# Softmax denominators issued pair by pair among the score matmuls of a causal attention layer

## The chip, the cores and the metric

The kernel runs on all 8 cores of one Trainium2 chip. Each core computes one element of a batch of 8, with the same program and no exchange between cores. The metric is device time in microseconds of the slowest core. Each core has a matrix engine (TensorE, PE in the profile; its weight loads are the rows PEld), a vector engine (DVE), a scalar engine (ACT), a general engine (POOL) and a queue engine for transfers (SP). Each engine takes its own instructions in program order, and they wait for each other through semaphores.

## The reference

Per batch element, x is 2048 tokens by 2048 features. The layer is, in short:

```
ln  = layernorm(x)
q,k,v = ln @ W_Q[h] + b, ln @ W_K[h] + b, ln @ W_V[h] + b      # 16 heads of 128
scores = q @ k.T / sqrt(128);  keys after the query are masked out
attn   = softmax(scores);      z = attn @ v
x  = x + layernorm(sum over heads of z @ W_O[h] + b_O)
bw = sign(weight) * mean(|weight|, per row)
x  = x + layernorm(layernorm(x) @ bw.T + bias)
```

The softmax divides exp(score) by the sum over all keys of a query. That sum, the denominator, is what the change is about.

## The kernel before, in words

The program has three stages. The first normalises and transposes x and makes q, k and v of head 0. The second runs through 16 heads. The third binarises the second weight and does the output projection and the feed-forward part. Only the second stage is touched.

A head is worked through in four blocks of 512 queries (`g` = 0 to 3, `GQ` = 512). Since keys after a query are masked, block g needs 4(g+1) chunks of 128 keys: 4, 8, 12 and 16 chunks, 40 in a head. For each chunk j there is:

- a **score** matmul (`emit_score`, L569), 128 keys by 512 queries. Chunks j = 0, 1 modulo 4 land in the two halves of the PSUM tensor psA, chunks 2, 3 modulo 4 in psB;
- an **exp** on ACT (`emit_exp`, L583), one for a pair of chunks, since it reads all of psA or all of psB (`estep` = 2). It writes the pair's slots of the SBUF buffer `ptil`. The score matmul that next writes the same half waits for it;
- for the last four chunks of a block, which are the diagonal ones (r = 0 to 3), a **mask** on POOL: a memset of the first r*128 columns (L606) and a multiplication of the next 128 by a triangle (L609);
- a **denominator** matmul (L619): a matrix of ones times the slot, accumulated over all chunks of the block in the second bank of psC. It waits for the chunk's exp, or for its mask where there is one.

After the last denominator matmul, ACT takes Ln (L624) and Exp (L628) to form the reciprocal, DVE multiplies each slot by it (L638), and PE multiplies the slots by v into psE (L656, the AV matmuls). In the fourth block 64 matmuls of the next head's q projection (L362) stand between the denominators and the AV matmuls, and hide the reciprocal.

The order of each engine's work is the order in which the Python code emits it; there is no scheduler. For PE it is, around a block: scores of the block's first four chunks, the AV matmuls of the block before, the rest of the scores, then all denominator matmuls of the block in one row. At the end of a head, q, k and v of the next come with 192 projection matmuls, with a short chain that forms the shift of the softmax (`emit_mh_mms`, `emit_mh_tail`, `emit_mb`) and 16 transposes of v.

Of the kernel before, what the change touches and what calls it, by code (L numbers as in the profile page):

```python
# [10 lines left out]
ALU = mybir.AluOpType  # L11
# [49 lines left out]
def build_program(SEQ, DM, H):  # L61
# [7 lines left out]
    TPG = min(4, NT)  # L69
    NG = NT // TPG  # L70
    GQ = TPG * 128
# [5 lines left out]
    p = Plan(nc)  # L77
# [26 lines left out]
    ptil = nc.alloc_sbuf_tensor("ptil", [128, max(NT * GQ, 4 * DM)], BF16)  # L104
    C2 = nc.alloc_sbuf_tensor("c2", [128, max(6 * DM, 4 * GQ + SEQ + 4 * DM)], BF16)
    eye_sb = nc.alloc_sbuf_tensor("eye_sb", [128, 128], BF16)
    tri_sb = nc.alloc_sbuf_tensor("tri_sb", [128, 128], BF16)
# [9 lines left out]
    onem_sb = nc.alloc_sbuf_tensor("onem_sb", [128, 128], BF16)  # L117
# [15 lines left out]
    pslot = [ptil[:, j * GQ:(j + 1) * GQ] for j in range(NT)]  # L133
# [18 lines left out]
    psC = nc.alloc_psum_tensor("psC", [128, 1024], F32)  # L152
# [21 lines left out]
    for dst, src in ((eye_sb, eye_h), (tri_sb, tri_h), (onec_sb, onec_h),  # L174
# [3 lines left out]
             inc="CONST", incn=16)  # L178
# [115 lines left out]
    sc_rinv_prev = 0  # L294
# [215 lines left out]
    def emit_mb(h):  # L510
        nonlocal pe_mb_prev, dv_mbias, dv_mbias_prev
        pe_mb = p.op("tensor", lambda e: e.matmul(
            psC[:, 0:1], oner_sb[:], nm_bf[:], start=True, stop=True),
            wait=[("DV", dv_nm_cur), ("DV", dv_qkv_evac_d[(h, 1)]),
                  ("SC", sc_rinv_prev)], inc="PE")
        pe_mb_prev = pe_mb
        dv_mbias = p.op("vector", lambda e: e.tensor_copy(
            mbias[:], psC[:, 0:1]), wait=[("PE", pe_mb)], inc="DV")
        dv_mbias_prev = dv_mbias

    for h in range(H):
# [10 lines left out]
        if h >= wo_start:  # L532
# [3 lines left out]
            for hh in range(hh0, min(hh0 + per, H)):  # L536
                p.op("gpsimd", lambda e, hh=hh: e.dma_start(
                    Bz[:, hh * DM:(hh + 1) * DM], wo_h.ap()[hh]),
                    inc="WO", incn=16)
# [8 lines left out]
        wait = [("DV", dv_qkv_all), ("DV", dv_mx_d[1])]  # L548
# [11 lines left out]
        estep = 2 if GQ == 512 else 1  # L560

        def emit_score(g, j, pe_sc):
            hb = j % 4
            wait = [("SC", psbuf_last_rd[hb])]
            if j == 0:
                wait += [("DV", dv_vch[h]), ("DV", dv_qkv_all)]
                if g == 0:
                    wait.append(("DV", dv_mx_d[1]))
            pe_sc[j] = p.op("tensor", lambda e, j=j, g=g, hb=hb: e.matmul(  # L569
                schalf[hb], kt_sb[:, j * 128:(j + 1) * 128],  # L570
                qt_sb[:, g * GQ:(g + 1) * GQ], start=True, stop=True),
                wait=wait, inc="PE")

        def emit_exp(g, j0, pe_sc, sc_exp):
            if estep == 2:
                buf = psA[:] if (j0 % 4 == 0) else psB[:]
                dst = ptil[:, j0 * GQ:(j0 + 2) * GQ]
            else:
                buf = schalf[j0 % 4]
                dst = pslot[j0]  # L580
            wait = [("PE", pe_sc[j0 + estep - 1]), ("DV", dv_mbias),
                    ("PE", max(ptil_slot_av[j0:j0 + estep]))]
            t_exp = p.op("scalar", lambda e, buf=buf, dst=dst: e.activation(  # L583
                dst, buf, AF.Exp, bias=mbias[:, 0:1], scale=C_ATTN),
                wait=wait, inc="SC")
            for jj in range(j0, j0 + estep):
                sc_exp[jj] = t_exp
                psbuf_last_rd[jj % 4] = t_exp

        pe_sc = {}  # L590
        sc_exp = {}
        mb_done = False
        for j in range(TPG):
            emit_score(0, j, pe_sc)
            if (j + 1) % estep == 0:
                if not mb_done:
                    emit_mb(h)
                    mb_done = True
                emit_exp(0, j + 1 - estep, pe_sc, sc_exp)
        for g in range(NG):  # L600
            chunks = (g + 1) * TPG
            gp_mask_j = {}
            for r in range(TPG):
                j = g * TPG + r
                if r > 0:
                    p.op("gpsimd", lambda e, j=j, r=r: e.memset(  # L606
                        ptil[:, j * GQ:j * GQ + r * 128], 0.0),
                        wait=[("SC", sc_exp[j])], inc="GP")
                gp_mask_j[j] = p.op("gpsimd", lambda e, j=j, r=r: e.tensor_tensor(  # L609
                    ptil[:, j * GQ + r * 128:j * GQ + (r + 1) * 128],  # L610
                    ptil[:, j * GQ + r * 128:j * GQ + (r + 1) * 128],
                    tri_sb[:], ALU.mult), wait=[("SC", sc_exp[j])], inc="GP")
            pe_den = 0
            for j in range(chunks):
                wait = [("SC", sc_exp[j])] if j < g * TPG else \
                    [("GP", gp_mask_j[j])]
                if j == 0:
                    wait.append(("SC", sc_rinv_prev))
                pe_den = p.op("tensor", lambda e, j=j, chunks=chunks: e.matmul(  # L619
                    psC[:, 512:512 + GQ], onem_sb[:], pslot[j],  # L620
                    start=(j == 0), stop=(j == chunks - 1)),
                    wait=wait, inc="PE" if j == chunks - 1 else None)
            p.drain("scalar")
            p.op("scalar", lambda e: e.activation(  # L624
                psC[:, 512:512 + GQ], psC[:, 512:512 + GQ], AF.Ln,
                bias=0.0, scale=1.0), wait=[("PE", pe_den)])
            p.drain("scalar")
            sc_rinv = p.op("scalar", lambda e, g=g: e.activation(  # L628
                rbc[g % 2], psC[:, 512:512 + GQ], AF.Exp, bias=0.0, scale=-1.0),
                wait=[("DV", rbc_war[g % 2])], inc="SC",  # L630
                lowp="softmax normalizer becomes a bf16 matmul operand")
            sc_rinv_prev = sc_rinv
            dv_norm = {}
            for j in range(chunks):
                wait = [("SC", sc_rinv)] if j == 0 else []
                if j == 0:
                    wait.append(("PE", pe_den))
                dv_norm[j] = p.op("vector", lambda e, j=j, g=g: e.tensor_tensor(  # L638
                    pslot[j], pslot[j], rbc[g % 2], ALU.mult),
                    wait=wait, inc="DV")  # L640
            rbc_war[g % 2] = dv_norm[chunks - 1]
            nchunks = (g + 2) * TPG
            if g + 1 < NG:
                pe_sc = {}
                for j in range(min(4, nchunks)):
                    emit_score(g + 1, j, pe_sc)
            elif h + 1 < H:
                emit_w_mms(h + 1, 0)
                emit_mh_sq(0, h + 1)
            pe_av = 0  # L650
            for j in range(chunks):
                wait = [("DV", dv_norm[j])]
                if j == 0:
                    wait += [("DV", dv_zevac.get(gidx - 1, 0)),
                             ("SC", max(sc_bw_evac_half))]
                pe_av = p.op("tensor", lambda e, j=j, chunks=chunks: e.matmul(  # L656
                    psE[:, 0:GQ], v_sb[:, j * 128:(j + 1) * 128], pslot[j],
                    start=(j == 0), stop=(j == chunks - 1)),
                    wait=wait, inc="PE")
                ptil_slot_av[j] = pe_av  # L660
            pe_av_all[h] = pe_av
            if g + 1 < NG:
                sc_exp = {}
                for j0 in range(0, min(4, nchunks), estep):
                    emit_exp(g + 1, j0, pe_sc, sc_exp)
                for j in range(min(4, nchunks), nchunks):
                    emit_score(g + 1, j, pe_sc)
                    if (j + 1) % estep == 0 and j + 1 > 4:
                        emit_exp(g + 1, j + 1 - estep, pe_sc, sc_exp)
            zpar = gidx % 2  # L670
            wait = [("PE", pe_av), (ZWs[zpar], zw_par_t[zpar])]
            dv_zevac[gidx] = p.op("vector", lambda e, zpar=zpar: e.tensor_copy(
                zstage[zpar], psE[:, 0:GQ]), wait=wait, inc="DV")
            zw_par_t[zpar] = p.op(
                "sync", lambda e, g=g, h=h, zpar=zpar: e.dma_start(
                    zs_h.ap()[g * TPG:(g + 1) * TPG, h].transpose([1, 0, 2]),
                    zstage[zpar].rearrange("p (t q) -> p t q", q=128)),
                wait=[("DV", dv_zevac[gidx])], inc=ZWs[zpar], incn=16)
            gidx += 1
            if g == NG - 1 and h + 1 < H:  # L680
                emit_mh_mms(0, h + 1)
# [243 lines left out]
    for i in range(NT):  # L925
# [6 lines left out]
        if i > 0:  # L932
# [5 lines left out]
         wait=[("OUT0", p.cnt("OUT0"))])  # L938
# [14 lines left out]
def _get_nc():  # L953
    key = (_SEQ, _DM, _H)
    if key not in _nc_cache:
        _nc_cache[key] = build_program(*key)
    return _nc_cache[key]
# [30 lines left out]
```

How the kernel before makes its waits and increments, by code:

```python
        def thunk(e, fn=fn, wait=wait, inc=inc, incn=incn, lowp=lowp):  # L43
            for (s, v) in wait:
                e.wait_ge(sems[s][0], v)
            if lowp is not None:
                with nc.allow_low_precision(reason=lowp):
                    ins = fn(e)
            else:
                ins = fn(e)
            if inc is not None:
                ins.then_inc(sems[inc][0], incn)
```

## Time and profile before

| | |
|---|---|
| median of 3 runs | 2399.13 us (2398.44 to 2399.26) |
| the profiled execution, its own time | 2399.46 us |
| its span, first to last instruction, slowest core | 2397.6 us |
| mean granted TensorE clock of that core | 0.906 |
| cores | 2387.9 to 2397.6 us |
| PE busy | 1860.8 us, 78% |
| DVE busy | 936.9 us, 39% |
| ACT busy | 614.4 us, 26% |
| POOL busy | 239.7 us, 10% |

In the span cut in 40 slices the heads fill slices 8 to 30 or so, with PE busy 70 to 80% there, ACT 10 to 40% and POOL at most 10%. PE busy is that of instructions which overlap in part: a 128x512 matmul is shown with 0.38 us at the full clock, yet the next one starts 0.22 us later. The granted clock has two levels in this trace, 1.00 (2.4 GHz) and 0.50 (1.2 GHz).

### The profile page before, as it was taken

The page shows a single profiled execution, that of the slowest core. Times are in us where ns is not written, and L with a number is a line of the kernel's source. Part 1 is how long each engine was busy: PE and PEld are TensorE (multiplying, and loading weights), DVE is VectorE, ACT ScalarE, POOL GpSimd, SP SyncE. Part 2 cuts the span into 40 slices and gives each one's busy share as a digit, 9 for nine tenths or more (in the row PEclk, how much of TensorE's full clock was granted, in tenths as well). Part 3 has the DMA queues.
Part 4 walks back from the last instruction along what each step waited for, and adds up shares of the span by engine and source line. Part 5 has one row for each costly group of instructions (what it writes and reads, how often), then busy time and mean ns, then how long its engine had stood idle before and what let it go on. Part 6 is the DMA issues. An engine that isn't in the chain of part 4 may idle for free.

```text
span 2397.6 us, 27121 instructions; the slowest of 8 cores (2387.9 to 2397.6 us)
## 1 busy us (share of the span) xinstructions
PE 1860.8 (78%) x8180; PEld 805.4 (34%) x8336; DVE 936.9 (39%) x1696; ACT 614.4 (26%) x785; POOL 239.7 (10%) x558
## 2 busy tenths in 40 slices
PE   1556877878778787787878879788744799999995
PEld 1232323323233232332323323233222344444442
DVE  3443333323233333333333333333243455555553
ACT  1134042240412304133141331403254311111111
POOL 1001010110111101111010111111110000000000
PEclk9778998989889898898988989889866899999997
DMA  6231211202122121221312234242054033333320
GB/s 153 89 84 18 29 23 16 29 12 29 16 22 25 16 30 16 23 25 14 31 16 22 25 49 47 35 55 45 5 180 149 18 88 88 88 88 88 88 76 39
DMA packets 178474, 119.33 MB, mean 50 GB/s; under 512 B 168100, under 2 KB 168100, under 8 KB 170148
## 3 DMA queue, kind: packets, MB, share of 16 engines
q0 software_dynamic: 107200, 75.51, 18.2%
q1 hardware_dynamic: 71140, 42.07, 7.0%
q8 instruction: 79, 1.29, 0.2%
q14 instruction: 55, 0.45, 0.1%
HBM read 125.97 MB, written 25.17 MB: 63 GB/s over the span
## 4 chain that ended last, share of the span: by engine, by line
PE 64%; ACT 11%; issue 9%; DVE 8%; POOL 4%; DMA 2%; DVEq 2%; ACTq 0%; POOLq 0%; another core or an unknown queue 0%; SPq 0%
PE psA L362 9%; PE psB L362 9%; PE psE L656 7%; ACT ptil L583 6%; PE psC L362 5%; PE psC L853 5%; PE psB L744 4%; PE psA L744 4%; PE psC L619 3%; POOL ptil L609 2%; PE psE L853 2%; PE psD L853 2%; PE psD L362 2%; PE psE L362 2%; DMA c<-x 2%
## 5 line engine op out<-in xcount | busy, mean ns | idle before, releaser
L638 DVE TENSOR_TENSOR ptil<-ptil,c 128x512 bf16<-128x512 bf16 x640 | 220.2, 417 | 479.6 <-ACT c L628 479.6
L362 PE MATMUL psA<-arena_a,wbuf 128*128 128x512 bf16 x1002 | 299.5, 384 | 6.8 <-ACT arena_a L276 3.8
L362 PE MATMUL psB<-arena_a,wbuf 128*128 128x512 bf16 x1002 | 298.6, 383 | 5.0 <-ACT arena_a L276 4.0
L656 PE MATMUL psE<-ptil,v 128*128 128x512 bf16 x625 | 185.1, 390 | 53.5 <-DVE ptil L638 53.3
L583 ACT ACTIVATE ptil<-psA,mbias 128x1024 bf16<-128x1024 f32 x160 | 178.3, 1114 | 182.9 <-PE psE L656 78.0
L619 PE MATMUL psC<-ptil,onem_sb 128*128 128x512 bf16 x624 | 179.7, 400 | 54.3 <-POOL ptil L606 25.2
L487 ACT ACTIVATE srow<-srow 1x1 f32<-1x1 f32 x32 | 6.5, 203 | 821.3 <-DVE srow L482 821.3
L609 POOL TENSOR_TENSOR ptil<-ptil,tri_sb 128x128 bf16<-128x128 bf16 x256 | 109.1, 426 | 890.0 <-ACT ptil L583 889.9
L583 ACT ACTIVATE ptil<-psB,mbias 128x1024 bf16<-128x1024 f32 x160 | 177.2, 1107 | 0.0
L569 PE MATMUL psA<-qt,kt 128*128 128x512 bf16 x314 | 107.3, 425 | 81.4 <-ACT ptil L583 50.9
L853 PE MATMUL psC<-arena_a,c 128*128 128x512 bf16 x496 | 149.9, 381 | 17.6 <-DVE c L837 9.2
L362 PE MATMUL psC<-arena_a,wbuf 128*128 128x512 bf16 x538 | 156.8, 381 | 4.9 <-DVE qt L376 4.5
L362 PEld LDWEIGHTS psA<-arena_a,wbuf 128*128 128x128 bf16 x1024 | 101.1, 99 | 131.2 <-issue 16.6
L362 PEld LDWEIGHTS psB<-arena_a,wbuf 128*128 128x128 bf16 x1024 | 100.9, 99 | 125.4 <-issue 8.6
L569 PE MATMUL psB<-qt,kt 128*128 128x512 bf16 x315 | 108.4, 428 | 26.2 <-ACT ptil L583 25.9
L656 PEld LDWEIGHTS psE<-ptil,v 128*128 128x128 bf16 x640 | 62.3, 97 | 187.9 <-issue 153.1
L619 PEld LDWEIGHTS psC<-ptil,onem_sb 128*128 128x128 bf16 x640 | 62.6, 98 | 174.3 <-issue 125.0
L853 PE MATMUL psE<-arena_a,c 128*128 128x512 bf16 x256 | 97.5, 381 | 0.1
L853 PE MATMUL psD<-arena_a,c 128*128 128x512 bf16 x255 | 97.1, 381 | 0.0
L362 PE MATMUL psD<-arena_a,wbuf 128*128 128x512 bf16 x235 | 89.5, 381 | 4.9 <-issue 3.2
L362 PE MATMUL psE<-arena_a,wbuf 128*128 128x512 bf16 x231 | 88.0, 381 | 0.3
L376 DVE TENSOR_SCALAR kt<-psD,bqkvT_sb 128x512 bf16<-128x512 f32 x15 | 11.3, 751 | 191.2 <-PE psC L362 191.2
(124 smaller groups left out, 2136.6 us busy)
## 6 DMA issues: line engine op xcount, KB each, us to landing
c<-fw POOLq DMA_DIRECT2D x16, 1024.0 KB, 5.1
ptil<-x SPq DMA_DIRECT2D x16, 1024.0 KB, 6.6
out<-wbuf POOLq DMA_DIRECT2D x16, 1024.0 KB, 9.2
wbuf<-wq POOLq DMA_DIRECT2D x16, 512.0 KB, 7.1
wbuf<-wk POOLq DMA_DIRECT2D x16, 512.0 KB, 7.1
c<-x SPq DMA_DIRECT2D x8, 1024.0 KB, 5.4
wbuf<-wv POOLq DMA_DIRECT2D x16, 512.0 KB, 7.1
zs<-c SPq DMA_DIRECT2D x64, 128.0 KB, 1.9
```

The lines of the kernel that those rows point to most:

```text
L362: e.matmul(banks[bidx], wslot[sl][:, c * 128:(c + 1) * 128], ln1t3[:, c, s * SLW:(s + 1) * SLW], start=(c == 0), stop=(c == NCH - 1)),
L376: e.tensor_scalar(d[:, s * SLW:(s + 1) * SLW], banks[bidx], bqkvT_sb[:, wi * H + h:wi * H + h + 1], None, ALU.add), wait=[("PE", pe_mm)],
L487: t_ln = p.op("scalar", lambda e, wh=which: e.activation(srow[0:1, 18 + wh:19 + wh], srow[0:1, 16 + wh:17 + wh], AF.Ln, bias=0.0, scale=1. ...
L569: pe_sc[j] = p.op("tensor", lambda e, j=j, g=g, hb=hb: e.matmul(schalf[hb], kt_sb[:, j * 128:(j + 1) * 128], qt_sb[:, g * GQ:(g + 1) * GQ] ...
L583: t_exp = p.op("scalar", lambda e, buf=buf, dst=dst: e.activation(dst, buf, AF.Exp, bias=mbias[:, 0:1], scale=C_ATTN), wait=wait, inc="SC")
L609: gp_mask_j[j] = p.op("gpsimd", lambda e, j=j, r=r: e.tensor_tensor(ptil[:, j * GQ + r * 128:j * GQ + (r + 1) * 128], ptil[:, j * GQ + r * ...
L619: pe_den = p.op("tensor", lambda e, j=j, chunks=chunks: e.matmul(psC[:, 512:512 + GQ], onem_sb[:], pslot[j], start=(j == 0), stop=(j == ch ...
L638: dv_norm[j] = p.op("vector", lambda e, j=j, g=g: e.tensor_tensor(pslot[j], pslot[j], rbc[g % 2], ALU.mult), wait=wait, inc="DV")
L656: pe_av = p.op("tensor", lambda e, j=j, chunks=chunks: e.matmul(psE[:, 0:GQ], v_sb[:, j * 128:(j + 1) * 128], pslot[j], start=(j == 0), st ...
L744: p.op("tensor", lambda e, hh=hh, s=s, d=zrd: e.matmul(projb[s], d[:, hh * 128:(hh + 1) * 128], Bz[:, hh * DM + s * 512:hh * DM + s * 512 ...
L853: p.op("tensor", lambda e, c=c, s=s: e.matmul(ffnb[s], ln3t[:, c * 128:(c + 1) * 128], bwt3[:, c, s * 512:s * 512 + PSW], start=(c == 0), ...
```

## The change

In both versions the exps, the masks, the reciprocal, the multiplications and the AV matmuls are the same instructions. The masks and the denominator matmuls are now emitted behind the exp of their own pair, by two new functions, `emit_mask` and `emit_den`, and `emit_emd`, which calls all three.

```diff
+        def emit_den(g, j, sc_exp, gp_mask_j):
+            chunks = (g + 1) * TPG
+            wait = [("SC", sc_exp[j])] if j < g * TPG else \
+                [("GP", gp_mask_j[j])]
+            if j == 0:
+                wait.append(("SC", sc_rinv_prev))
+            pe_den_d[g] = p.op("tensor", lambda e, j=j, chunks=chunks:
+                               e.matmul(psC[:, 512:512 + GQ], onem_sb[:],
+                                        pslot[j], start=(j == 0),
+                                        stop=(j == chunks - 1)),
+                               wait=wait,
+                               inc="PE" if j == chunks - 1 else None)
+
+        def emit_emd(g, j0, pe_sc, sc_exp, gp_mask_j):
+            emit_exp(g, j0, pe_sc, sc_exp)
+            for jj in range(j0, j0 + estep):
+                if jj >= g * TPG:
+                    emit_mask(g, jj, sc_exp, gp_mask_j)
+                emit_den(g, jj, sc_exp, gp_mask_j)
...
-                emit_exp(0, j + 1 - estep, pe_sc, sc_exp)
+                emit_emd(0, j + 1 - estep, pe_sc, sc_exp, gp_mask_j)
         for g in range(NG):
             chunks = (g + 1) * TPG
-            gp_mask_j = {}
-            for r in range(TPG):
...
-            pe_den = 0
-            for j in range(chunks):
...
+            pe_den = pe_den_d[g]
...
                 for j0 in range(0, min(4, nchunks), estep):
-                    emit_exp(g + 1, j0, pe_sc, sc_exp)
+                    emit_emd(g + 1, j0, pe_sc, sc_exp, gp_mask_j)
                 for j in range(min(4, nchunks), nchunks):
                     emit_score(g + 1, j, pe_sc)
                     if (j + 1) % estep == 0 and j + 1 > 4:
-                        emit_exp(g + 1, j + 1 - estep, pe_sc, sc_exp)
+                        emit_emd(g + 1, j + 1 - estep, pe_sc, sc_exp,
+                                 gp_mask_j)
```

The waits of each instruction are as before. On ACT, DVE, POOL and SP the order of the instructions is as before too; only PE's order differs. On PE, first in the first two blocks of head 0 before (L551 the transposes of v, L569 scores, L512 the shift, L619 denominators, L656 AV matmuls):

```order
L551 MATMUL psA<-eye_sb,ptil 128x128 x16
L569 MATMUL psA<-qt,kt 128x512 x2
L512 MATMUL psC<-nm_bf,oner_sb 128x1
L569 MATMUL psB<-qt,kt 128x512 x2
L619 MATMUL psC<-ptil,onem_sb 128x512 x4
L569 MATMUL psA<-qt,kt 128x512 x2
L569 MATMUL psB<-qt,kt 128x512 x2
L656 MATMUL psE<-ptil,v 128x512 x4
L569 MATMUL psA<-qt,kt 128x512 x2
L569 MATMUL psB<-qt,kt 128x512 x2
L619 MATMUL psC<-ptil,onem_sb 128x512 x8
```

The same place on PE now (L608 is the denominator matmul, L669 the AV matmul):

```order
L569 MATMUL psA<-qt,kt 128x512 x2
L512 MATMUL psC<-nm_bf,oner_sb 128x1
L608 MATMUL psC<-ptil,onem_sb 128x512 x2
L569 MATMUL psB<-qt,kt 128x512 x2
L608 MATMUL psC<-ptil,onem_sb 128x512 x2
L569 MATMUL psA<-qt,kt 128x512 x2
L569 MATMUL psB<-qt,kt 128x512 x2
L669 MATMUL psE<-ptil,v 128x512 x4
L608 MATMUL psC<-ptil,onem_sb 128x512 x4
L569 MATMUL psA<-qt,kt 128x512 x2
L608 MATMUL psC<-ptil,onem_sb 128x512 x2
L569 MATMUL psB<-qt,kt 128x512 x2
```

Each pair of denominator matmuls stands directly behind the scores that feed its exp, and ahead of the next pair of scores. The four denominators of a block's first four chunks, whose scores are issued ahead of the AV matmuls, come together behind those.

On PE at the end of the fourth block, before, where the last scores, the row of denominators and the first projection matmuls (L362) of the next head stand:

```order
L569 MATMUL psA<-qt,kt 128x512 x2
L569 MATMUL psB<-qt,kt 128x512 x2
L619 MATMUL psC<-ptil,onem_sb 128x512 x16
L362 MATMUL psA<-arena_a,wbuf 128x512 x2
L362 MATMUL psB<-arena_a,wbuf 128x512 x2
```

The same place on PE now:

```order
L608 MATMUL psC<-ptil,onem_sb 128x512 x2
L569 MATMUL psA<-qt,kt 128x512 x2
L608 MATMUL psC<-ptil,onem_sb 128x512 x2
L569 MATMUL psB<-qt,kt 128x512 x2
L608 MATMUL psC<-ptil,onem_sb 128x512 x2
L362 MATMUL psA<-arena_a,wbuf 128x512 x2
```

The row of 16 is gone: two denominators stand at its place, and the others alternate with pairs of scores through the block.

## Rows read from the trace of the kernel before

**Rows 1.** The page: chain that ended last by engine; denominator matmuls.
```profile
PE 64%; ACT 11%; issue 9%; DVE 8%; POOL 4%; DMA 2%; DVEq 2%; ACTq 0%; POOLq 0%; another core or an unknown queue 0%; SPq 0%
...
L619 PE MATMUL psC<-ptil,onem_sb 128*128 128x512 bf16 x624 | 179.7, 400 | 54.3 <-POOL ptil L606 25.2
```

**Rows 2.** Timeline, fourth block: start, duration (us), engine, line, operation, [idle before <-releaser].
```profile
527.63 3.62 PE L656 MATMUL psE<-ptil,v 128*128 128x512 bf16 x11 [1.26 <-DVE ptil L638]
...
531.42 0.59 PE L569 MATMUL psA<-qt,kt 128*128 128x512 bf16 x2 [0.17 <-issue]
...
532.22 1.11 ACT L583 ACTIVATE ptil<-psA,mbias 128x1024 bf16<-128x1024 f32 x1 [1.77 <-PE psA L569]
...
533.48 0.59 PE L569 MATMUL psA<-qt,kt 128*128 128x512 bf16 x2 [1.03 <-ACT ptil L583]
...
536.98 3.61 PE L619 MATMUL psC<-ptil,onem_sb 128*128 128x512 bf16 x16
537.35 1.11 ACT L583 ACTIVATE ptil<-psB,mbias 128x1024 bf16<-128x1024 f32 x1
...
539.59 0.43 POOL L609 TENSOR_TENSOR ptil<-ptil,tri_sb 128x128 bf16<-128x128 bf16 x1
...
540.69 0.58 ACT L624 ACTIVATE psC<-psC 128x512 f32<-128x512 f32 x1 [2.23 <-PE psC L619]
540.71 0.59 PE L362 MATMUL psA<-arena_a,wbuf 128*128 128x512 bf16 x2
```

**Rows 3.** Timeline, first block of the same head.
```profile
500.01 1.12 ACT L583 ACTIVATE ptil<-psA,mbias 128x1024 bf16<-128x1024 f32 x1 [4.30 <-DVE mbias L517]
...
501.82 0.41 POOL L609 TENSOR_TENSOR ptil<-ptil,tri_sb 128x128 bf16<-128x128 bf16 x1
...
503.84 0.58 PE L619 MATMUL psC<-ptil,onem_sb 128*128 128x512 bf16 x1 [0.16 <-POOL ptil L609]
...
504.22 1.06 PE L569 MATMUL psA<-qt,kt 128*128 128x512 bf16 x2
...
505.07 1.06 PE L569 MATMUL psB<-qt,kt 128*128 128x512 bf16 x2
```

**Rows 4.** Timeline, second block, and the ends of the third.
```profile
508.38 1.11 ACT L583 ACTIVATE ptil<-psB,mbias 128x1024 bf16<-128x1024 f32 x1
...
508.63 0.59 PE L569 MATMUL psA<-qt,kt 128*128 128x512 bf16 x2 [0.69 <-ACT ptil L583]
...
510.44 1.11 ACT L583 ACTIVATE ptil<-psB,mbias 128x1024 bf16<-128x1024 f32 x1
...
512.68 0.42 POOL L609 TENSOR_TENSOR ptil<-ptil,tri_sb 128x128 bf16<-128x128 bf16 x1
...
513.25 0.38 PE L619 MATMUL psC<-ptil,onem_sb 128*128 128x512 bf16 x1 [0.36 <-POOL ptil L609]
...
515.87 2.61 PE L656 MATMUL psE<-ptil,v 128*128 128x512 bf16 x8 [1.26 <-DVE ptil L638]
...
525.00 0.38 PE L619 MATMUL psC<-ptil,onem_sb 128*128 128x512 bf16 x1 [0.37 <-POOL ptil L609]
```

**Rows 5.** Stretches: busy us of each engine (instructions), granted clock, DMA share, GB/s.
```profile
core 2: us, PE busy (x) PEld busy (x) DVE busy (x) ACT busy (x) POOL busy (x), PEclk, DMA share, GB/s
502.00:506.50 4.50, 3.84 (x8) 0.85 (x8) 0.51 (x2) 1.31 (x3) 1.67 (x5) 0.50 0.00 0
506.60:508.00 1.40, 1.27 (x4) 0.38 (x4) 0.82 (x3) 0.63 (x1) 0.00 (x0) 1.00 0.00 0
532.00:534.00 2.00, 0.97 (x5) 0.19 (x2) 0.45 (x1) 1.78 (x2) 0.00 (x0) 1.00 0.27 61
558.00:561.00 3.00, 1.53 (x5) 0.38 (x4) 2.76 (x4) 0.00 (x0) 0.00 (x0) 1.00 1.56 152
561.20:564.50 3.30, 3.30 (x9) 1.26 (x9) 1.25 (x3) 0.20 (x1) 0.00 (x0) 0.50 0.23 34
564.60:566.00 1.40, 1.40 (x8) 0.62 (x7) 0.00 (x0) 0.00 (x0) 0.00 (x0) 1.00 0.00 0
```

More of the change, by code:

```diff
@@ L588, in emit_exp, with emit_mask @@
                 psbuf_last_rd[jj % 4] = t_exp
+        def emit_mask(g, j, sc_exp, gp_mask_j):
+            r = j - g * TPG
+            if r > 0:
+                p.op("gpsimd", lambda e, j=j, r=r: e.memset(
+                    ptil[:, j * GQ:j * GQ + r * 128], 0.0),
+                    wait=[("SC", sc_exp[j])], inc="GP")
+            gp_mask_j[j] = p.op("gpsimd", lambda e, j=j, r=r: e.tensor_tensor(
+                ptil[:, j * GQ + r * 128:j * GQ + (r + 1) * 128],
+                ptil[:, j * GQ + r * 128:j * GQ + (r + 1) * 128],
+                tri_sb[:], ALU.mult), wait=[("SC", sc_exp[j])], inc="GP")
+        def emit_den(g, j, sc_exp, gp_mask_j):
[16 more added lines that the diff above has]
+                emit_den(g, jj, sc_exp, gp_mask_j)
         pe_sc = {}
         sc_exp = {}
+        gp_mask_j = {}
+        pe_den_d = {}
         mb_done = False
@@ L598, in build_program @@
                     mb_done = True
-                emit_exp(0, j + 1 - estep, pe_sc, sc_exp)
+                emit_emd(0, j + 1 - estep, pe_sc, sc_exp, gp_mask_j)
         for g in range(NG):
             chunks = (g + 1) * TPG
-            gp_mask_j = {}
-            for r in range(TPG):
[L604 to L612, printed above, removed]
-            pe_den = 0
-            for j in range(chunks):
[L615 to L622, printed above, removed]
+            pe_den = pe_den_d[g]
             p.drain("scalar")
@@ L663, in build_program @@
                 sc_exp = {}
+                gp_mask_j = {}
                 for j0 in range(0, min(4, nchunks), estep):
-                    emit_exp(g + 1, j0, pe_sc, sc_exp)
+                    emit_emd(g + 1, j0, pe_sc, sc_exp, gp_mask_j)
                 for j in range(min(4, nchunks), nchunks):
```

## The prediction

> **What bounds the kernel now.** I read the chain of waits first. Two thirds of it are PE, 11% ACT and 4% POOL, and DMA is 2% [rows 1]: the kernel is bound by PE's queue and by the places where that queue stands waiting, not by transfers. Then I read the timeline of one head, which the 16 heads repeat, at the places where PE waits within the attention blocks.
>
> In the fourth block [rows 2] the reader is to see two engines that overlap. ACT starts its exps 1.03 us apart ((537.35 - 532.22)/5). PE needs 0.59 us for the pair of scores that feeds one, and then idles: 1.03 us ahead of the pair at 533.48, which waits for the exp that frees psA. Two score buffers are enough to keep ACT fed, since the next scores are made in one while ACT reads the other. Behind the last scores the 16 denominator matmuls run without a gap, in 3.61 us, or 0.216 us each. They end at 540.59, and PE goes on with the next head at 540.71. So PE's queue alone sets the pace from here. The last mask ended at 540.02, so that not even a PE with nothing else to do could have ended the denominators much before 540.5.
>
> In the first two blocks the last denominator waits for POOL's last mask: it starts at 503.84 and 513.25, each time behind a mask, as the third block's at 525.00 does [rows 3, 4]. The row of denominators costs hardly anything on the path there.
>
> **The change part by part.** PE takes its matmuls in the order written. The work on every engine is the same as before: 640 denominator matmuls and 640 scores. What is added is a wait in a bad place: a denominator pair waits for the exp (or the mask) of the scores directly ahead of it, and the next scores are queued behind it, though their buffer is free. ACT waits for those scores. The overlap of scores with exps is gone for every pair but the first two of a block.
>
> The step that takes its place, at the full clock, from [rows 2]: two scores until the end of the second, 0.59; to ACT's start 0.21 (532.22 - 532.01); exp 1.11; back to PE 0.15 (533.48 - 533.33); two denominators issued, 0.43. That is 2.49 us a pair, against the 1.03 us of ACT's pace and the pair's 0.43 us in the row of denominators behind.
>
> A diagonal pair waits for its mask. For r = 0, 1 the second mask ends 1.10 us behind the exp (501.82 + 0.41 against 500.01 + 1.12) [rows 3]; for r = 2, 3 it is 1.55 us (512.68 + 0.42 against 510.44 + 1.11) [rows 4]. PE starts some 0.12 us after a mask. The first diagonal pair takes 0.59 + 0.21 + 1.11 + 1.10 + 0.12 + 0.22 = 3.35 us, the last, to the end of its last matmul, 0.59 + 0.21 + 1.11 + 1.55 + 0.15 + 0.38 = 3.99 us.
>
> From the end of the AV matmuls of the block before to the end of the last denominator:
>
> - Fourth block: four denominators 0.86, four plain steps 9.96, the diagonal ones 3.35 and 3.99: 18.2 us. Before: 531.25 to 540.59 = 9.3. Added: 8.8.
> - Third block: 0.86 + 4.98 + 3.35 + 3.99 = 13.2 us. Before: 518.48 to 525.38 = 6.9. Added: 6.3.
> - Second block: the denominators of chunks 2 and 3 wait for the exp that ends at 509.49, so scores that ran at 508.63 start at 509.64 + 0.43 = 510.07; the two diagonal pairs lead to 517.4. Before: 513.63. Added: 3.8 [rows 4].
> - First block, at the low clock (issue 0.43 a matmul, a pair of scores 1.06, from [rows 3]): the second denominator starts behind the mask at about 502.35; scores 502.8 to 503.8, exp 504.0 to 505.1, mask until 506.7, last denominator until 507.3. Before: 504.42. Added: 2.9.
>
> That is 21.8 us a head, with nothing beside it: in the first three blocks reciprocal, DVE and AV matmuls hang on the last denominator, and in the fourth the 64 projection matmuls are queued behind it on PE. The later start of an AV row hides nothing. Sixteen heads: 349 us. POOL's weight loads are queued behind the masks of the head before and so come later with everything else; transfers have no part in the chain worth a price here.
>
> **The clock.** TensorE's granted clock is at 0.50 through 502 to 506.5 although PE is busy 3.84 of 4.50 us, and rises only then; it is 1.00 from 558 to 561, with PE busy 1.53 of 3.00 us (some five matmuls), and is at 0.50 right behind [rows 5]. At 532 to 534 PE was busy 0.97 of 2.00 us and kept the full clock. A step of the new order has four matmuls, some 1.2 of 2.49 us, 48% in this measure, just where rows of both kinds stand; the diagonal steps have about 35%. So I expect falls within the blocks. At the low clock a step is 1.06 + 0.21 + 1.11 + 0.15 + 0.86 = 3.39 us, 0.90 more, with PE busy about 60% of it, less than the 85% that went ahead of the rise. Once fallen, the clock then stays low until the AV row or the projections. There are 12 steps in the last three blocks. I take four of them at the low clock: 3.6 us. The projections behind the fourth block mostly start at the low clock and need what those behind 561.2 needed, about 3.3 us at half pace, which loses 1.7 us. Together 5.3, and so 27.1 us a head, 434 us in all.
>
> The page "TensorE: Matmul & The Clock Gate" of the Trainium skill (Part 1, and "HAM oscillation") has a rule that speaks for less: it ties the fall to a stretch in which the engine is idle throughout. No part of the new blocks is such a stretch, since each step has four matmuls, so by that rule the clock stays up. The fall behind 561 is against it, since PE had five matmuls in the 3 us before. By that rule alone the time would be that of the second case below.
>
> The sum is made against the profiled execution, 2399.5 us (span 2397.6), which is 0.3 us above the median of the runs. 2399.5 + 434 = 2833 us.
>
> The bounds: all 12 steps at the full clock and the projections too, 349 us, 2748 us. All 12 at the low clock: 10.8 + 1.7 for the projections, and 2.6 us for the three rows of four denominators, 36.9 us a head, 590 us, 2990 us. I stay near the middle of the lower half, since each AV row is dense and gives the full clock back to the steps behind it.
>
> **The rivals.**
>
> 1. The serial order as above, the clock falls for part of the steps: 2833 us, 2770 to 2900. For it: the order of PE, and the rows of the clock.
> 2. The same, but the clock stays at its upper level: 2748 us (2735 to 2770). For it: 532 to 534. Against it: the fall behind 561 and the sparse diagonal steps.
> 3. The same, but the low clock nearly throughout, which also slows the AV rows: 2900 to 2990 us. Against it: at 506.6 the clock is up just as an AV row begins, and it would be so again.
> 4. The other side: the denominators fill the gaps in which PE waits for ACT. That needs PE to go on with the next scores while a denominator waits, from the moment at which scores can be started ahead of a waiting matmul. Each gap has 1.03 us of idle time and a pair needs 0.43. But the price is small even then: masks end at 540.02, the denominator behind them at 540.02 + 0.12 + 0.38 = 540.52 instead of 540.59, and the other blocks wait for masks already, so 0.07 us a head, 1 us. Only an earlier rise of the clock in the first block could add to that, by 1.7 us a head, which is 27 us: 2371 to 2399 us. Against it: in all rows a waiting matmul holds those behind it, as the scores at 533.48 hold the row of denominators, whose first twelve inputs were ready long before. The same page (Part 2, on loading the stationary operand) says that only weight loads are pulled ahead and matmuls stay in program order, with which these rows agree.
> 5. The order doesn't change what it says: PE's order shows that it does, so this has no chance of its own.
>
> **How the numbers follow.** Case 1 has 0.80, case 2 has 0.10, case 3 has 0.07, case 4 has 0.03. The time is that of case 1, 2833 us. A range of 2745 to 2900 holds cases 1 and 2 nearly whole. All cases but the fourth are far slower than before; about 0.2% (5 us) is what a measurement can tell from no change. Slower: 0.97. Within 0.2%: 0.01. Faster: 0.02.
>
> **What would show it.** In the changed kernel's fourth block ACT's exps should start some 2.5 us apart at the full clock and 3.4 at the low one, not 1.03, each releasing a denominator matmul (L608) that is followed by two scores (L569) without a wait. The wait of ACT for PE's scores should rise to hundreds of microseconds. POOL's diagonal masks should release denominators with scores behind them. The mean granted clock should fall from 0.906 to about 0.83. A head should take some 27 us longer, with the growth largest in its fourth block. If exps stay 1.03 us apart, the first term is wrong; if the steps are 2.5 us but the granted clock stays near 0.9, case 2 holds.

## The result and the profile after

The changed kernel is slower. Its median is 2859.8 us over 10 runs, that of the kernel before 2399.2 us over 10 runs beside it; the ratio is 1.192, with a 95% interval of 1.190 to 1.193. The forecast was 2833 us, in a range of 2745 to 2900. (In some executions the cores of one or both dies show a lower granted clock than the others and take longer; the ratios, and the medians given below, leave these out.)

| | before | after |
|---|---|---|
| span of the profiled execution, us | 2397.6 | 2856.8 |
| PE busy, us | 1860.8 (78%) | 2028.6 (71%) |
| mean granted clock, slowest core | 0.906 | 0.806 |
| ACT's share of the chain that ended last | 11% | 14% |

The page of the changed kernel shows the chain by engine, and then the groups for denominators, exps and scores (count, then busy us, mean ns of one, then idle us ahead of them and what ended most of it):

```profile
PE 63%; ACT 14%; issue 8%; DVE 7%; POOL 4%; DMA 2%; DVEq 1%; ACTq 1%; POOLq 0%; SPq 0%
...
L608 PE MATMUL psC<-ptil,onem_sb 128*128 128x512 bf16 x640 | 273.8, 491 | 459.7 <-ACT ptil L583 164.9
...
L583 ACT ACTIVATE ptil<-psA,mbias 128x1024 bf16<-128x1024 f32 x160 | 178.3, 1114 | 341.9 <-PE psA L569 180.0
L583 ACT ACTIVATE ptil<-psB,mbias 128x1024 bf16<-128x1024 f32 x160 | 177.9, 1112 | 255.4 <-PE psB L569 255.4
...
L569 PE MATMUL psA<-qt,kt 128*128 128x512 bf16 x320 | 142.5, 540 | 27.0 <-DVE v L557 27.0
...
L569 PE MATMUL psB<-qt,kt 128*128 128x512 bf16 x320 | 147.5, 557 | 0.0
```

The same groups for exps and scores before:

```profile
L583 ACT ACTIVATE ptil<-psA,mbias 128x1024 bf16<-128x1024 f32 x160 | 178.3, 1114 | 182.9 <-PE psE L656 78.0
...
L583 ACT ACTIVATE ptil<-psB,mbias 128x1024 bf16<-128x1024 f32 x160 | 177.2, 1107 | 0.0
L569 PE MATMUL psA<-qt,kt 128*128 128x512 bf16 x314 | 107.3, 425 | 81.4 <-ACT ptil L583 50.9
...
L569 PE MATMUL psB<-qt,kt 128*128 128x512 bf16 x315 | 108.4, 428 | 26.2 <-ACT ptil L583 25.9
```

PE's idle time ahead of denominators was 54.3 us [rows 1] and is 459.7 us, 405 us more. Part of that replaces waits that stood ahead of scores, 108 us before and 27 now. All in all PE is not busy for 828 us of the span instead of 537, which is 291 us of the loss; the other 168 us are its busy time, which grew though the work is the same. ACT's exps are as fast as before (1.11 us), but they wait 435 us for scores; the exps from psB had no wait at all before. A denominator matmul's mean went from 400 to 491 ns, which is the clock: one alone is shown with 0.38 us at the full clock and with 0.58 or 0.59 at the low one.

The timeline of a fourth block shows the cycle (start, duration, engine, operation, idle time before and what ended it; weight loads and transfers are left out). It answers to [rows 2].

```profile
634.62 0.59 PE L569 MATMUL psA<-qt,kt 128*128 128x512 bf16 x2
635.43 1.11 ACT L583 ACTIVATE ptil<-psA,mbias 128x1024 bf16<-128x1024 f32 x1 [2.27 <-PE psA L569]
636.68 0.59 PE L608 MATMUL psC<-ptil,onem_sb 128*128 128x512 bf16 x2 [1.47 <-ACT ptil L583]
637.12 0.59 PE L569 MATMUL psB<-qt,kt 128*128 128x512 bf16 x2
637.92 1.11 ACT L583 ACTIVATE ptil<-psB,mbias 128x1024 bf16<-128x1024 f32 x1 [1.38 <-PE psB L569]
639.17 1.01 PE L608 MATMUL psC<-ptil,onem_sb 128*128 128x512 bf16 x2 [1.47 <-ACT ptil L583]
...
641.25 1.11 ACT L583 ACTIVATE ptil<-psA,mbias 128x1024 bf16<-128x1024 f32 x1 [2.22 <-PE psA L569]
...
644.58 1.11 ACT L583 ACTIVATE ptil<-psB,mbias 128x1024 bf16<-128x1024 f32 x1 [2.22 <-PE psB L569]
...
654.73 0.58 PE L608 MATMUL psC<-ptil,onem_sb 128*128 128x512 bf16 x1 [0.16 <-POOL ptil L596]
655.27 1.01 PE L362 MATMUL psA<-arena_a,wbuf 128*128 128x512 bf16 x2
```

The reader is to see a loop of two engines, each of which now waits for the other: PE 1.47 us for the exp, ACT 1.38 us for the scores. From 635.43 to 637.92 is 2.49 us, the step of the prediction. From 641.25 to 644.58 it is 3.33 us. The clock has fallen by then: the pair at 639.17 takes 1.01 us instead of 0.59. The projections at 655.27 still run at the low clock.

The stretches of the same head, from the second block on, cut where the granted clock changes (busy us of PE, its weight loads, DVE, ACT and POOL with the number of instructions, then the clock, the share of the DMA engines and GB/s):

```profile
597.40:604.10 6.70, 3.17 (x12) 0.96 (x10) 0.69 (x1) 3.17 (x3) 0.95 (x3) 1.00 0.10 22
604.20:610.90 6.70, 3.93 (x9) 1.13 (x10) 1.73 (x6) 2.29 (x3) 1.44 (x4) 0.50 0.01 1
611.00:617.70 6.70, 3.96 (x16) 1.34 (x14) 1.64 (x4) 3.95 (x4) 0.00 (x0) 1.00 0.08 20
617.90:631.40 13.50, 8.19 (x18) 2.24 (x19) 2.15 (x7) 3.93 (x6) 2.39 (x7) 0.50 0.00 0
631.50:638.20 6.70, 4.74 (x19) 1.63 (x17) 2.55 (x7) 3.05 (x4) 0.00 (x0) 1.00 0.08 20
638.30:658.70 20.40, 12.12 (x27) 3.52 (x28) 1.82 (x6) 6.37 (x7) 3.54 (x8) 0.50 0.14 14
658.80:661.00 2.20, 2.20 (x12) 0.98 (x10) 2.20 (x8) 0.00 (x0) 0.00 (x0) 1.00 1.06 104
```

In each of these three blocks the clock came up while the AV matmuls of the block before ran (from 609.85 and 629.92, and those of the first block) and fell a few steps later. In the steps at the low clock PE is busy about 60% of the time and the clock stayed low; it rose again where matmuls followed each other closely.

Where the time went, by the starts of ACT's first exp and its four Ln's in each head, mean of the first 15 heads over the 8 cores:

| us a head | before | after | growth |
|---|---|---|---|
| first exp to Ln of block 1 | 4.5 | 7.5 | 3.0 |
| to Ln of block 2 | 9.4 | 13.6 | 4.2 |
| to Ln of block 3 | 11.8 | 20.0 | 8.2 |
| to Ln of block 4 | 15.2 | 27.1 | 11.9 |
| to the first exp of the next head | 59.8 | 61.3 | 1.5 |

The sum of the growths is 28.8 us, and 16 heads make 461 us.

### The profile page after: what moved, and what is told of

Same layout as the page of the kernel before. It is cut to its first block, busy times and chain, and to the rows that moved or that the text cites. A ratio compares the mean times of both kernels' runs of the same rounds, so it can differ in the third digit from the quotient of the medians.

```text
span 2856.8 us, 27277 instructions; the slowest of 8 cores (2847.5 to 2856.8 us)
## 1 busy us (share of the span) xinstructions
PE 2028.6 (71%) x8336; PEld 827.9 (29%) x8336; DVE 936.9 (33%) x1696; ACT 630.2 (22%) x785; POOL 239.4 (8%) x558
## 4 chain that ended last, share of the span: by engine, by line
PE 63%; ACT 14%; issue 8%; DVE 7%; POOL 4%; DMA 2%; DVEq 1%; ACTq 1%; POOLq 0%; SPq 0%
ACT ptil L583 10%; PE psA L362 8%; PE psB L362 8%; PE psC L608 7%; PE psE L669 5%; PE psC L362 4%; PE psA L759 4%; PE psC L868 4%; PE psB L759 4%; PE psB L569 3%; PE psA L569 3%; POOL ptil L596 2%; PE psE L868 2%; PE psD L868 2%; PE psD L362 2%
## 5 line engine op out<-in xcount | busy, mean ns | idle before, releaser
L608 PE MATMUL psC<-ptil,onem_sb 128*128 128x512 bf16 x640 | 273.8, 491 | 459.7 <-ACT ptil L583 164.9
L362 PE MATMUL psA<-arena_a,wbuf 128*128 128x512 bf16 x1024 | 320.1, 401 | 3.1 <-ACT arena_a L276 3.1
L362 PE MATMUL psB<-arena_a,wbuf 128*128 128x512 bf16 x1024 | 317.4, 398 | 3.2 <-ACT arena_a L276 3.2
L608 PEld LDWEIGHTS psC<-ptil,onem_sb 128*128 128x128 bf16 x640 | 64.3, 100 | 686.8 <-issue 675.5
L669 PE MATMUL psE<-ptil,v 128*128 128x512 bf16 x640 | 189.2, 429 | 28.6 <-DVE ptil L651 28.6
L569 PE MATMUL psA<-qt,kt 128*128 128x512 bf16 x320 | 142.5, 540 | 27.0 <-DVE v L557 27.0
L362 PE MATMUL psC<-arena_a,wbuf 128*128 128x512 bf16 x544 | 157.2, 379 | 4.5 <-DVE qt L376 4.5
L569 PE MATMUL psB<-qt,kt 128*128 128x512 bf16 x320 | 147.5, 557 | 0.0
L362 PEld LDWEIGHTS psA<-arena_a,wbuf 128*128 128x128 bf16 x1024 | 104.2, 102 | 140.4 <-issue 32.7
L362 PEld LDWEIGHTS psB<-arena_a,wbuf 128*128 128x128 bf16 x1024 | 104.4, 102 | 136.4 <-issue 26.6
L669 PEld LDWEIGHTS psE<-ptil,v 128*128 128x128 bf16 x640 | 64.5, 101 | 175.9 <-issue 140.6
L362 PE MATMUL psD<-arena_a,wbuf 128*128 128x512 bf16 x240 | 90.9, 379 | 4.5 <-issue 3.6
L362 PE MATMUL psE<-arena_a,wbuf 128*128 128x512 bf16 x240 | 90.9, 379 | 0.0
L759 PE MATMUL psA<-arena_b,kt 128*128 128x512 bf16 x256 | 77.9, 386 | 3.4 <-ACT c L782 3.4
```

Of the source, the lines that this page charges most:

```text
L362: e.matmul(banks[bidx], wslot[sl][:, c * 128:(c + 1) * 128], ln1t3[:, c, s * SLW:(s + 1) * SLW], start=(c == 0), stop=(c == NCH - 1)),
L608: e.matmul(psC[:, 512:512 + GQ], onem_sb[:], pslot[j], start=(j == 0), stop=(j == chunks - 1)),
L759: p.op("tensor", lambda e, hh=hh, s=s, d=zrd: e.matmul(projb[s], d[:, hh * 128:(hh + 1) * 128], Bz[:, hh * DM + s * 512:hh * DM + s * 512 ...
```

## The experiments

In all of them `emit_emd` of the changed kernel is edited. In all but one, a list `pend` holds the denominators that are not yet issued, and `flush_den(keep)` issues all but the last `keep` pairs; it is called with 0 at a block's end. The one without it adds matmuls instead.

```diff
-                emit_den(g, jj, sc_exp, gp_mask_j)
+                pend.append((g, jj, sc_exp, gp_mask_j))
+            flush_den(KEEP)
+        def flush_den(keep):
+            while len(pend) > keep * estep:
+                emit_den(*pend.pop(0))
```

**Denominators two pairs late** (`KEEP` = 2).

> Each denominator pair is issued two pairs later than in the changed kernel: behind the scores of the pair after next's exp buffer, so that its exp is done when PE comes to it; the last two pairs stand at the block's end. As many denominators are interleaved as two fewer pairs a block allow. Theory (the wait ahead of the next scores is the cause, not the interleaving): exps are 1.03 us apart again, the last denominator ends 0.5 us behind the last mask as before; 2395 to 2405 us. Rival (interleaving itself costs, by switching PE between two kinds of matmuls and two PSUM banks): each of 12 pairs a head between scores keeps a cost of at least 0.2 us, 192 pairs, so over 2435 us.

Measured: ratio to before 1.0067 (1.0050 to 1.0084), median 2413.9 against 2397.7 us. The wait is gone and with it 96% of the loss. The rival's cost of 0.2 us a pair is not there: in the trace one, three and five pairs of denominators stand between scores in blocks 2, 3 and 4, 144 in all (the expectation's 192 count those behind a block's last scores too), and they would have cost 29 us. But 16 us are left, and 2414 lies above the theory's 2405. The cores of this run tell where they come from (span, mean granted clock):

```profile
core 0: 2410.7 us, clock 0.892
...
core 4: 2403.2 us, clock 0.897
core 5: 2395.6 us, clock 0.906
core 6: 2391.6 us, clock 0.906
...
```

Time follows the clock: the two cores at 0.906, the value of before, have spans of 2391.6 and 2395.6 us, like those of before (2387.9 to 2397.6). The same stretch of one head on core 0, and below it on core 6:

```profile
707.40:714.10 6.70, 4.33 (x17) 1.44 (x16) 0.69 (x1) 4.37 (x5) 2.40 (x7) 1.00 0.09 20
714.30:720.90 6.60, 5.79 (x15) 1.79 (x14) 3.46 (x9) 3.12 (x5) 0.00 (x0) 0.50 0.01 2
```

```profile
708.20:714.90 6.70, 4.49 (x17) 1.53 (x16) 0.69 (x1) 4.53 (x5) 2.39 (x7) 1.00 0.09 20
715.10:721.70 6.60, 5.17 (x20) 1.92 (x20) 3.46 (x9) 4.60 (x5) 0.00 (x0) 1.00 0.10 22
```

Almost the same work goes ahead in both; on core 0 the clock falls as the second block's reciprocal is made, and the next stretch does 15 matmuls instead of 20. So on core 6 the interleaving costs nothing that can be told from noise: a head takes 100.8 us there and 100.7 before. A likely reason for the fall on core 0, not tested by itself, is that the interleaving takes matmuls out of the row that had stood ahead of that gap.

**Denominators one pair late** (`KEEP` = 1).

> Each denominator pair is issued one pair later than in the changed kernel, behind the next pair of scores. Theory: the chain from one exp to the one that uses the same buffer becomes 1.11 + 0.15 + 0.43 (denominators) + 0.59 + 0.21 = 2.49 us for two pairs, 1.25 us a pair where ACT alone needs 1.03; 0.22 us for some 10 to 12 pairs a head and 16 heads: 35 to 42 us, 2430 to 2450 us. No diagonal wait is ahead of scores, and the clock stays up as before. Rival (interleaving itself costs): as for the version with two pairs, the same in both.

Measured: 2464.1 us, a single execution and so without an interval, with cores from 2450.7 to 2462.5 us. That is 14 us over the expected 2450. A stretch of the fourth block on core 0 has the period of the theory:

```profile
650.89 1.11 ACT L583 ACTIVATE ptil<-psA,mbias 128x1024 bf16<-128x1024 f32 x1 [2.36 <-PE psA L569]
...
652.15 0.59 PE L608 MATMUL psC<-ptil,onem_sb 128*128 128x512 bf16 x2 [0.60 <-ACT ptil L583]
652.58 0.59 PE L569 MATMUL psA<-qt,kt 128*128 128x512 bf16 x2
...
653.38 1.11 ACT L583 ACTIVATE ptil<-psA,mbias 128x1024 bf16<-128x1024 f32 x1 [0.37 <-PE psA L569]
...
655.87 1.11 ACT L583 ACTIVATE ptil<-psA,mbias 128x1024 bf16<-128x1024 f32 x1 [0.37 <-PE psA L569]
```

The exps into the same buffer are 2.49 us apart (650.89, 653.38, 655.87), two pairs as expected, and the scores between them do not wait for a mask. A head takes 105.0 us on this core against 100.7 before, so 4.3 us where 2.6 was expected. The clock, assumed to stay up, did not: the trace's clock record has 2.3, 1.8 and 2.7 us a head more of blocks 2 to 4 at the low level than before on the same core. At half pace these 6.8 us can hold at most 3.4 us of lost work; how much of them is on the path was not measured. Of the 4.3 us, 0.7 lie behind the fourth Ln, where the theory had none, and stay unexplained.

**Extra matmuls in the gaps of the changed kernel**, to keep PE active.

```diff
+            if g > 0 and j0 >= 4:      # psD <- qt,kt, 128x512, results unread
+                emit_fill(3 if j0 < g * TPG else (4 if j0 == g * TPG else 5))
+            for jj in range(j0, j0 + estep):
                 emit_den(g, jj, sc_exp, gp_mask_j)
```

> The changed kernel with extra matmuls, whose results nobody reads, into the unused PSUM tensor psD while PE would wait for an exp or a mask: 3 ahead of a plain denominator pair, 4 and 5 ahead of the diagonal ones, in blocks 2 to 4 only, 48 a head. Theory (7 us a head of the loss is the low clock that the sparse steps bring): steps stay 2.49 us, the clock stays at its upper level through the blocks, the projections behind the fourth block start fast; 2735 to 2765 us, some 110 us faster than the changed kernel although PE has 768 matmuls more. Rival (the steps are longer for another reason, or the clock falls all the same): no faster than 2860 us, and up to 40 us slower.

Measured: ratio 1.1514 (1.1474 to 1.1554), which is 2761 us; the fastest run is 2752.6 us. The edit adds 9, 15 and 21 matmuls in blocks 2, 3 and 4, so 45 a head and 720 in all, not the 48 and 768 of the expectation (the trace shows 718). In the profiled execution six of the eight cores have 2744.3 to 2752.5 us. The other two, cores 6 and 7, have 2773 us, by three heads with 65 to 68 us from the fourth Ln to the next exp instead of 59.8. Their granted clock shows why. For 251 us in all, 135 of them in these three stretches, it stood at a third value, 0.81, which no other core of this run had. The stretch from 1370 to 1424 us on core 6 and, below it, on core 5:

```profile
1370.00:1424.00 54.00, 50.10 (x186) 20.37 (x188) 15.80 (x26) 0.20 (x1) 2.29 (x2) 0.81 0.24 24
```

```profile
1370.00:1424.00 54.00, 45.43 (x209) 20.25 (x207) 18.92 (x32) 1.09 (x4) 2.29 (x2) 0.93 0.21 22
```

Core 6 does 186 matmuls where core 5 does 209. What brought that value is not known. Adding work made the kernel some 98 us faster by the ratio, and 107 us by the fastest run. The third block on core 0, where every step has the full clock:

```profile
589.77 1.11 ACT L583 ACTIVATE ptil<-psA,mbias 128x1024 bf16<-128x1024 f32 x1 [1.38 <-PE psA L569]
591.03 0.59 PE L614 MATMUL psC<-ptil,onem_sb 128*128 128x512 bf16 x2 [0.82 <-ACT ptil L583]
591.46 0.59 PE L569 MATMUL psB<-qt,kt 128*128 128x512 bf16 x2
591.89 0.81 PE L592 MATMUL psD<-qt,kt 128*128 128x512 bf16 x3
592.26 1.11 ACT L583 ACTIVATE ptil<-psB,mbias 128x1024 bf16<-128x1024 f32 x1 [1.38 <-PE psB L569]
...
594.75 1.11 ACT L583 ACTIVATE ptil<-psA,mbias 128x1024 bf16<-128x1024 f32 x1 [1.38 <-PE psA L569]
```

The exps stay 2.49 us apart (589.77, 592.26, 594.75), and PE's wait is 0.82 us instead of 1.47 because three unread matmuls (L592) fill the rest. The four blocks of a head (the first four lines of the table above) now grow, against before on the same core, by 3.0, 4.0, 6.2 and 9.1 us, and the fifth line by nothing. With the clock up through blocks 3 and 4 that measures the serial part nearly alone: 22.3 us a head, where the prediction had 21.8.

**Only the fourth block interleaved** (`KEEP` = 0 in block 4, 99 elsewhere).

> Only the fourth block of each head interleaved as in the changed kernel; the first three with the row of denominators as before. Theory (each block pays its own price): the fourth block's 12.0 us and 1.5 us of slow projections a head, 16 heads, 216 us: 2600 to 2630 us. Rival (the blocks act on each other, the clock of one falling into the next, so that one alone costs much less than its share): under 2590 us.

Measured: ratio 1.0886 (1.0870 to 1.0902), 2609.5 us. The fourth block takes 26.7 us from Ln to Ln and the way to the next exp 61.4, about as in the changed kernel, with 27.1 and 61.3; the first three are those of before within 0.3 us. The blocks pay separately.

**Plain denominators at once, diagonal ones at the block's end** (`KEEP` = 0 for pairs without a mask, 99 for those with one).

> Plain denominators (no mask) issued at once as in the changed kernel, the four diagonal ones of a block in a row at its end, where their masks hold no scores. Theory, by the terms of the prediction: the first block is as before; second block +1.4 us; third 0.86 + 2 x 2.49 + 0.80 + 1.11 + 1.03 + 2.08 = 10.9 us against 6.9, +4.0; fourth 15.8 against 9.3, +6.5; 11.9 us a head, and 2 to 5 us for the low clock: 2399 + 16 x 13.9 to 16.9 = 2620 to 2670 us. So the mask waits would be worth some 190 to 240 us of the 460. Rival (the mask waits count little, since masks are waited for at a block's end in any order): over 2750 us.

Measured: ratio 1.1015 (1.0978 to 1.1052), which is 2643 us. So 217 us of the 460 come from diagonal denominators that stood ahead of scores, and the loss of the first block is all of that kind. The expectation calls this the worth of the mask waits, which is too much. The edit takes away the wait for the diagonal pair's exp too, and the low clock of a core goes from 1082 to 1106 us down to 727 to 751. What the mask adds to a step can be read in the changed kernel, at the first diagonal pair of the head above:

```profile
600.03 0.59 PE L569 MATMUL psA<-qt,kt 128*128 128x512 bf16 x2
...
603.40 0.59 PE L569 MATMUL psB<-qt,kt 128*128 128x512 bf16 x2
```

The step is 3.37 us instead of 2.49, so 0.88 us more, four times a head. By my estimate from these two numbers the masks alone are some 56 us of the 217. ACT's exps in a fourth block of this run:

```profile
704.39 1.11 ACT L583 ACTIVATE ptil<-psA,mbias 128x1024 bf16<-128x1024 f32 x1 [2.79 <-PE psA L569]
706.88 1.11 ACT L583 ACTIVATE ptil<-psB,mbias 128x1024 bf16<-128x1024 f32 x1 [1.38 <-PE psB L569]
709.37 1.11 ACT L583 ACTIVATE ptil<-psA,mbias 128x1024 bf16<-128x1024 f32 x1 [1.38 <-PE psA L569]
711.86 1.11 ACT L583 ACTIVATE ptil<-psB,mbias 128x1024 bf16<-128x1024 f32 x1 [1.38 <-PE psB L569]
715.19 1.11 ACT L583 ACTIVATE ptil<-psA,mbias 128x1024 bf16<-128x1024 f32 x1 [2.21 <-PE psA L569]
716.21 1.11 ACT L583 ACTIVATE ptil<-psB,mbias 128x1024 bf16<-128x1024 f32 x1
```

Three plain steps are 2.49 us long, the one to 715.19 is 3.33 (low clock), and the last exp follows after 1.02 us, since nothing waits between the diagonal pairs.

**The rows of before, with extra matmuls where PE waits.** These are put ahead of a head's scores too, into psD, from operands that don't change in this stage (`onem_sb` and `arena_a`). `emit_warm(n)` emits n of them: 10 behind the projection matmuls of v, 3 ahead of the transposes of v, 6 behind these, 4 ahead of block 1's denominators, and 2, 4 and 4 behind the first scores of blocks 2, 3 and 4.

```diff
             emit_w_mms(h, 2)
+            emit_warm(10, [("DV", dv_qkv_evac_d[(h, 1)])])
...
+            emit_warm(3)
...
+        emit_warm(6, [("SC", sc_evacA[NT - 1])])
...
+            if g == 0:
+                emit_warm(4)
...
+                emit_warm(2 if g == 0 else 4)
```

> The kernel before (rows of denominators at a block's end) with extra matmuls, whose results nobody reads, into the unused psD while PE waits: 10 and 3 around the norm matmuls of k, 6 ahead of a head's scores, 4 ahead of the first block's denominators, 2, 4 and 4 while the reciprocal is made. Theory (the low clock at a head's start costs PE time on the path: 16 transposes at 0.12 us and the scores and denominators of block 1 at half pace): the clock stays up through a head's start, 15 to 25 us less than before: 2375 to 2390 us. Rival (the extra matmuls delay what follows them, or the clock falls there all the same): 2399 us or more.

Measured: ratio 0.9933 (0.9911 to 0.9956), median 2383.6 us. Faster than before by 0.7%, 16 us by the ratio, as expected. The low clock adds up to 201 to 263 us a core instead of 434 to 451. Where the time came from is not what the theory said. From a fourth Ln to the next first exp a head has 58.8 us where before has 59.8, and that is the whole gain. The first block, now nearly always at the full clock, goes from 4.50 to 4.33 us, the second from 9.43 to 9.33, and the fourth grows by 0.3. The end of a first block on core 7, all of it at the full clock, shows why so little:

```profile
494.82 0.42 POOL L606 TENSOR_TENSOR ptil<-ptil,tri_sb 128x128 bf16<-128x128 bf16 x1
...
495.39 0.38 PE L618 MATMUL psC<-ptil,onem_sb 128*128 128x512 bf16 x1 [0.36 <-POOL ptil L606]
...
495.86 0.58 ACT L656 ACTIVATE psC<-psC 128x512 f32<-128x512 f32 x1 [2.17 <-PE psC L618]
```

The last denominator still waits for the last mask, as in [rows 3]; only its own 0.58 us became 0.38.

**Two pairs late, with the same extra matmuls.**

> The version with denominators two pairs late and the same extra matmuls. Theory (what that version lost, 15 us, was only the clock's fall in the third block of some cores; its wait costs nothing): as the rows with the same extra matmuls within 5 us, 2372 to 2392 us, on all cores alike. Rival (the interleaving costs by itself): 12 us or more above them.

Measured: ratio 0.9918 (0.9897 to 0.9939), median 2380.3 us, the fastest version here. The 16 us that this order lost without them are gone. The expectation wanted all cores alike, and they are not: their spans go from 2361.3 to 2376.5 us, with clocks from 0.958 to 0.943. The interval overlaps that of the one above, so which of the two orders is better is open; against before both are faster, by under 1%.

## Why the prediction was right, point by point

**What bounds the kernel, and the serial step.** Right. The step is 2.49 us at the full clock, and each of PE and ACT waits for the other in it. The prediction's 2.9, 3.8, 6.3 and 8.8 us for the four blocks are 3.0, 4.0, 6.2 and 9.1 us where the clock is kept up by extra matmuls. Two pairs of delay in the issue take the loss away.

**The diagonal waits.** Right in kind and size: the step with the first diagonal pair was put at 3.35 us and took 3.37 at the full clock. With all diagonal denominators taken out of the scores' way, 217 us come back, the masks' own share being smaller. Of the growth, 3.0 us in the first block are of this kind alone.

**The clock.** The mechanism was right, the size too small. I took four of 12 steps at the low clock and 1.7 us for slow projections, 5.3 us a head. The changed kernel less the version with extra matmuls, on core 0 of each, is 129.5 - 122.9 = 6.6 us a head: 0.2, 2.0 and 2.8 us in blocks 2 to 4, and 1.6 us for the projections. The four-step term is what was mis-sized: 5.0 us are six steps' worth of 0.84 us each (3.33 less 2.49, where 0.90 was predicted), not four. By blocks that is a third of a step in the second, 2.4 of four steps in the third and 3.3 of six in the fourth. The clock's 1.3 us a head over the forecast make 21 us and the serial part's 0.5 us a head 8 us, together 29 against the 27 us by which the forecast was short. The time is near the forecast, then, because most of it is the serial part; that four steps were taken rather than six was a guess that no row of before sizes. A mean clock of 0.83 was expected and 0.806 came.

**The rule of the clock page.** By what the Trainium skill's "TensorE: Matmul & The Clock Gate" (Part 1) says of idle stretches the clock would have stayed up, 2748 us. In the changed kernel it fell at 604.1, 617.8 and 638.2, with a dozen matmuls in the 6.7 us ahead of the first fall and at most 2.0 us between them; the measured time is 112 us above that case. The trace does not agree with the rule as a test for sparse activity.

**The rivals.** Case 2 is the changed kernel with extra matmuls, 2761 us, or 2753 at its fastest, against the 2748 predicted, so it measures what the clock decides. Case 3 fell because the clock came up in every head while AV rows ran: on every core each third and fourth block has 6.8 us or more at the full clock. Case 4, that gaps could take the denominators for at most 1 us of gain, is borne out from the other side: with the waits taken out of the way by two pairs, the cores whose clock is that of before have its time, not less. Its 1.7 us a head, 27 us, from an earlier rise of the clock in the first block name no row and were far too much: with the clock up there, the first two blocks of a head gained 0.3 us, since the last mask ends the first one at either clock. The 16 us of that version came from the way to the next head's first exp. One reading in this case is loose, too. The first twelve inputs of the row of denominators were not ready long before: the sixth exp, at about 535.3, ended some 0.6 us ahead of the row at 536.98. The argument needs only that some were ready while scores waited, and it stands.

## What to carry to other kernels

On an engine that takes its instructions in order, issue a consumer at least as many steps behind its producer as there are buffers between them; against the row at the block's end, none behind cost 19% here, one pair some 2.7%, and two pairs, one for each score buffer, 0.7%. Other numbers of buffers were not tried. Filling a gap in the timeline is only worth something if what is put there is ready when the gap opens, and if the work that it relieves ended the stage at all: here, in three blocks of four, masks did. Before an issue order is changed, write down for each waiting instruction what is queued behind it and who waits for that.

## What the runs showed of the hardware

The clock is part of an order's price, also where matmuls never stop for long. With 720 unread matmuls added, the changed kernel became some 98 us faster; the kernel before became 16 us faster with 33 a head. The same program with nearly the same timing fell to 1.2 GHz in the third block on core 0, from the sixth head on, and kept 2.4 GHz there on core 6, and the two cores ended 19 us apart. In another run two cores had a clock of 0.81 for 251 us and ended 20 to 29 us behind the other six. Before a difference between cores is put down to data or transfers, their granted clocks should be compared.
